# Two transformer layers on one core: whole-array jobs ahead of the values in TensorE's step

## What is computed

```python
xn = _layernorm(x)
x = x + _L0_attn_ref(xn, ...) + _L0_ffn_ref(xn, ...)
xn = _layernorm(x)
x = x + _L1_attn_ref(xn, ...) + _L1_ffn_ref(xn, ...)
```

## Time and profile before

| | |
|---|---|
| median of 3 runs | 901.5 us (899.99 to 901.91) |
| the profiled execution | 900.29 us, of which the profile's span is 897.3 us |
| TensorE, matmuls | 822.3 us busy, 92% of the span |
| TensorE, weight loads (beside matmuls) | 297.3 us, 33% |
| ScalarE | 762.6 us, 85% |
| VectorE | 540.9 us, 60% |
| GpSimd | 25.0 us, 3% |
| DMA | 76.07 MB, 85 GB/s on average |
| granted TensorE clock, mean | 0.966 |

### The profile page before, as it was taken

How to read it: one execution, slowest core, us unless ns; L and a number is a source line. 1 busy time by engine, 2 the same in 40 slices (tenths; PEclk the granted TensorE clock), 3 DMA queues, 4 the chain that set the end, 5 groups by cost and what they waited for, 6 DMA issues and landing times. The chain is left out here.

```text
span 897.3 us, 17912 instructions
## 1 busy us (share of the span) xinstructions
PE 822.3 (92%) x6815; PEld 297.3 (33%) x6815; DVE 540.9 (60%) x1193; ACT 762.6 (85%) x850; POOL 25.0 (3%) x39
## 2 busy tenths in 40 slices
PE   9568888899899999999899999999999789999996
PEld 7212222243233323333233323333233322333332
DVE  7165468675865567755866467846767167277321
ACT  1458998788989998899989998899988599899985
POOL 1000000000000000000000000000000000000000
PEclk9669998999999999999999999999999699999999
DMA  3663515533437307280246407280154604105100
GB/s 87 142 145 90 85 22 158 128 49 54 129 75 143 52 2 203 57 137 4 103 101 136 59 1 202 49 139 10 72 133 111 84 1 143 35 18 166 39 12 12
DMA packets 43889, 76.07 MB, mean 85 GB/s; under 512 B 6496, under 2 KB 8416, under 8 KB 43792
## 3 DMA queue, kind: packets, MB, share of 16 engines
q1 hardware_dynamic: 42492, 71.53, 36.1%
q10 hardware_dynamic: 668, 1.25, 0.8%
q0 software_dynamic: 640, 2.10, 0.7%
HBM read 37.37 MB, written 35.65 MB: 81 GB/s over the span
## 5 line engine op out<-in xcount | busy, mean ns | idle before, releaser
L664 ACT ACTIVATE probs<-ps_s 128x1024 f32<-128x1024 f32 x768 | 725.6, 1047 | 87.4 <-PE ps_s L810 87.0
L829 PE MATMUL ps_pv<-probs,v_aug 128*32 128x512 f32 x3072 | 419.4, 619 | 9.9 <-ACT probs L664 5.3
L810 PE MATMUL ps_s<-q_ab,k_ab 18*128 18x512 f32 (+1 forms) x1088 | 145.4, 507 | 35.3 <-ACT probs L664 23.1
L810 PEld LDWEIGHTS ps_s<-q_ab,k_ab 18*128 18x128 f32 (+1 forms) x1088 | 55.4, 186 | 207.7 <-ACT probs L664 165.8
L829 PEld LDWEIGHTS ps_pv<-probs,v_aug 128*32 128x32 f32 x3072 | 62.0, 109 | 119.0 <-issue 85.2
L689 PE MATMUL ps_misc<-h_hi,k_w 128*128 128x512 f32 x192 | 86.4, 450 | 2.6 <-DVE norm_max L1119 0.8
L810 PE MATMUL ps_s<-q_c,k_c 34*128 34x512 f32 x448 | 84.9, 453 | 0.0
L1217 DVE STREAM_TRANSPOSE pv_sb<-ps_pv 128x512 f32<-128x512 f32 x48 | 34.4, 716 | 71.6 <-PE ps_pv L829 68.5
L690 PE MATMUL ps_misc<-h_lo,k_w 128*128 128x512 f32 x192 | 76.6, 399 | 0.0
L1050 DVE CAST h_hi<-ff_out 128x512 fp32r<-128x512 f32 x64 | 27.3, 427 | 78.4 <-ACT ff_out L629 76.5
L689 PEld LDWEIGHTS ps_misc<-h_hi,k_w 128*128 128x128 f32 x192 | 36.3, 189 | 88.8 <-issue 45.2
(11 more groups left out here) (139 smaller groups left out, 555.0 us busy)
## 6 DMA issues: line engine op xcount, KB each, us to landing
parts_dram<-qk_parts SPq DMA_DIRECT2D x32, 512.0 KB, 3.4
parts_dram<-qk_parts SPq DMA_DIRECT2D x62, 256.0 KB, 4.0
q_ab<-parts_dram SPq DMA_DIRECT2D x64, 128.0 KB, 4.5
k_ab<-parts_dram SPq DMA_DIRECT2D x60, 128.0 KB, 5.9
q_c<-parts_dram SPq DMA_DIRECT2D x14, 512.0 KB, 7.6
k_c<-parts_dram SPq DMA_DIRECT2D x14, 512.0 KB, 9.0
x_all<-in_L_attn_x_dram SPq DMA_DIRECT2D x8, 256.0 KB, 6.5
out_dram<-x_all POOLq DMA_DIRECT2D x8, 256.0 KB, 6.7
```

The source lines that it names most:

```text
L664: nc.scalar.activation(probs[:, U.slot(s), 2 * half:2 * half + 2], ps_s[:, 2 * pair:2 * pair + 2], ACT.Exp, scale=SCALE[U.layer]).then_inc ...
L810: ins = nc.tensor.matmul(ps_s[:, bank, :], k[row:row + n, slot, c * P:(c + 1) * P], q[row:row + n, slot, :], start=True, stop=True)
L829: ins = nc.tensor.matmul(ps_pv[32 * j:32 * j + 32, :], v_aug[:, U.v, c, a:a + 32], probs[:, U.slot(s), j, :], start=c == 0 and not odd, st ...
```

## The change

In TensorE's program the jobs of a step are looked at before its values. In every unit but the first, the leading jobs that stand in the new list `WHOLE` are run between the scores and the values of the step; from the first job on that does not stand there, all stay behind the values. No table and no other engine's program is changed.

```diff
+WHOLE = ("x_t0", "x_t1", "quant_t", "ff_t", "w_t", "ff0", "ff1", "ff1_b", "ff2", "ff2_b")
...
                     items = TABLE[u].get(s, [])
                     exact = items and items[0][0] in ("exact0", "exact1")
                     holds = heads_within(int(items[0][0][-1]), items[0][1]) if exact else None
+                    jobs = [item for item in items if item[0] in TAKER or item[0] in ("exact0", "exact1")]
+                    n = 0
+                    while u > 0 and n < len(jobs) and jobs[n][0] in WHOLE:
+                        n += 1
+                    run(jobs[:n])
                     if s >= 2:
                         pv(U, s - 2)
                     elif u > 0:
                         pv(Unit(u - 1), STEPS - 2 + s)
-                    run(items, holds)
+                    run(jobs[n:], holds)
```

## The result

The changed kernel takes 919.99 us (median of 6 runs, 919.19 to 924.9) where the kernel before takes 901.14 (6 runs beside it, 899.99 to 902.23): ratio 1.022, 95% interval 1.0198 to 1.0242, slower. The forecast was 916.9, its likeliest case 911 to 922. The profiled execution took 924.9 us, of which the span is 922.2.

What follows compares the result with a forecast made beforehand. TensorE (92% busy) and ScalarE's exponentials take turns as the bound. Terms 2.0 + 1.3 + 4.5 + 0.9 + 7.8 - 1.1 = +15.4 us on the profiled 900.3 give 915.7; from the median 901.5, 916.9, range 905 to 926.

Steps and rivals of the forecast that it cites:

- the body of 103.9 to 104.1 us: Sign that the forecast is right: one loop body takes 103.9 to 104.1 us for 102.1.
- ff0 2, +0.9 five times: Loop body, step 4: its bank holds q1 until VectorE's shuffle ends, so job and values start late; 4.5 us in all.
- x_t1, +0.5 four times: Step 14 of C: the job waits for the normalised input and step 15's exponential has no reserve; 2.0 us in all.
- ff0 1, +0.25: Loop body, step 1: 0.6 idle until an activation empties its bank; +0.25 (0.15 to 0.4), five times, 1.3 us.
- ff1 1 and ff1 2, 0.2: Steps 14 and 0: the activation freeing the bank ends about 0.1 late; 2 x 0.1, five times, 0.9 to 1.0 us.
- The places that lose all of the cover: Outside the body, five jobs (three ff0, an x_t1, ff0 3) lose the whole cover of 1.0 us each.
- The seven shorter ones: Seven shorter losses outside the loop body, 0.1 to 0.8 us each, 2.8 together.
- Evictions on ScalarE, 0: The activations' 20.9 us wait for their jobs goes, but TensorE sets the exponential behind them, so nothing is gained.
- The rival that priced it as a gain, 896.0: ScalarE is what counts: the 20.9 us before the activations are on the path and come back, 896.0 us; chance 0.06.
- Tiling, 0 with ends of 16.7: Moved steps keep three changes of tiling, so 0; ends 111 x 0.15 = 16.7 us either way.
- ff1_b and ff_t in steps 1: They delay VectorE's take by 1.1 and 0.6, hidden by reserves; if those go, each costs up to 0.2 us.
- The case of the falling clock, 0.12: Rival: new idle time brings stretches at half clock, 1 to 3 us each; five to ten give 925 to 935; chance 0.12.

Runs made afterwards that it cites:

- the ready jobs alone: Kernel before, with only the 31 leading whole-array jobs whose bank and operands are ready in time moved (26 steps, units 5 to 17): 901.26 us, ratio 1.0008.
- ff1_b 2 alone: Kernel before, with only ff1_b 2 in step 1 of B moved ahead of the values (five times): 901.17 us for 899.92, ratio 1.0018.
- the copy first: Changed kernel, with VectorE's copy of x_t0 put ahead of the first part of the quantisation in step 3 of B: 916.85 us, ratio 1.0178.
- the steps 1 left as before: Changed kernel, but no job moved ahead of the values in any step 1 (15 steps): 911.85 us, ratio 1.0134.
- unit 1: Kernel before, with only x_t0 of unit 1, step 0 moved ahead of the values: 900.33 us, ratio 0.999.
- a close relative: Changed kernel, but ff0 2 of step 4 in five A units stays behind the values; run twice: 913.35 and 914.26 us, ratios 1.0146 and 1.0136.

## Why the prediction was right, and where not

The total was right (919.99 for 916.9, range 905 to 926), and so was the mechanism, time lost where a moved job waits with no values beneath it. Not all the terms were, and that the total came so close is in part luck: a missed term of 4.4 stands against terms that were 2.5 too dear. Of the signs named beforehand one failed, the body of 103.9 to 104.1 us (104.8); the others came.

- **ff0 2, +0.9 five times:** right, 0.89 each, the job at the end of the shuffle.
- **x_t1, +0.5 four times:** right, 0.57. **ff0 1, +0.25:** 0.36, inside its bounds. **ff1 1 and ff1 2, 0.2:** 0.17.
- **The places that lose all of the cover:** +0.89 in step 15 of units 2 and 19, +1.00 in unit 22, 0.84 in unit 4, 0.9 for ff0 3 in unit 17. Right. **The seven shorter ones**, 2.8 together, were too dear: the traces show some 1.6 at full clock, in units 4, 18, 20 and 21. One more, in step 9 of unit 20, shows as 0.69 in four kernels with a part undone, and not in either profile of the changed kernel, which has a fall of the clock 7 us before it.
- **Evictions on ScalarE, 0:** right. 15.2 of the 20.9 us went from ahead of the activations, and the exponentials' idle grew by 40.3. The rival that priced it as a gain, 896.0, is out.
- **Tiling, 0 with ends of 16.7:** right, by the ready jobs alone.
- **The term that failed: "ff1_b and ff_t in steps 1 delay VectorE's take behind them ... what hides that is a reserve".** I followed the take to the layer norm, found 0.7 of slack before x_t0 needs it, and stopped. The queue behind the take goes on: split, reciprocal, quantisation, then the copy out of x_t0's bank, on which q0 waits. That reserve was nothing. 0.88 for 0, at most 0.2, in five units: 4.4 us, shown by ff1_b 2 alone and by the copy first. ff_t's take cost 0.13 (C, step 3), within the bound. Unit 4 has a late take of its own, 0.34 by the steps 1 left as before.
- **A gain that I didn't see:** step 10 of A, -0.27 four times. The copy of v1's bank stands behind VectorE's split of ff0 3, and starts 1.40 after v1 before (444.47 to 445.87) and 1.13 after it in the changed kernel (457.56 to 458.69). That isn't the move of ff0 3. In the kernel with only ff0 2 behind the values again, ff0 3 is still moved, and the copy is as late as before, 1.40 after v1 (449.75), and the norm waits 1.09:

```profile
449.91 0.43 DVE L1057 CAST h_hi<-ff_out 128x512 fp32r<-128x512 f32 x1
...
451.15 0.69 DVE L1123 COPY v_aug<-ps_misc 128x512 f32<-128x512 f32 x1
...
451.90 0.39 PE L733 MATMUL ps_misc<-qk_sq,head_sel 128*32 128x512 bf16 x2 [1.09 <-DVE v_aug L1123]
```

It belongs to ff0 2: its 0.89 delays TensorE and the exponentials, but VectorE's rotation of q1 and k1 less, so that VectorE comes to the split of ff0 3 earlier against them (0.19 ahead of v1's start, 457.37, for 0.16 behind it). So ff0 2 cost 0.89 less 0.27 in four bodies.

Added up at full clock, with the loop's terms times their places: 2.3 (x_t1) + 1.8 (ff0 1) + 3.4 (ff0 2 less step 10) + 0.9 (ff1) + 0.4 (C) + 4.4 (B) + 6.4 (outside, for 7.8: 4.5 in the five places, 1.6 in the shorter ones, 0.3 behind unit 4's take) - 1.1 = 18.5, against 18.85 between the medians. So the forecast was 3.1 short: one missed chain of 4.4, for the greater part made up by the gain in step 10 (1.1) and by places outside the body that were too dear (1.4). The case of the falling clock, 0.12, came true in part: more falls, but outside the body. The six runs were at half clock for 66 us at the median, by span and granted clock, the two profiles for 76 and 62, and that of before for 61. Inside the body the clock stayed whole in both profiles of the changed kernel, in spite of waits of 1.03 in step 4 and 0.81 before the norm.

## What to carry to other kernels

In the program of an engine that works in order, as TensorE's does here, filler work (the values) belongs beneath a wait: between a job and the one that needs it, or ahead of a job whose bank or input comes late. Which tile shape stood first was no criterion here. Before a job is moved ahead of filler, compare the time at which its bank and its input are ready with the filler's start; only if both are there is the move free, and it gains only if something waits for its result. And when a move delays one instruction on another engine (a take), follow that engine's queue to the first result that someone waits for, not only the result that the instruction itself makes: here 0.87 of the 1.00 reached the exponential. Compare such kernels step by step in their traces where the clock is whole: here that tells 0.06 us, and the runs tell 2 to 3.

## What the runs showed of the hardware

In two profiles of the changed kernel, 4.9 us apart, the steps' exponentials add the same within 0.06 us from unit 4 to 16, where the granted clock is 1.00; the difference arises in the first 170 us, where the stretches at 0.50 lie differently (129.9 and 160.6 in the one, one of 17.1 us from 149.0 in the other). In the profile before, stretches at 0.50 sum to 61 us of 897. Three of the other kernels (the ready jobs, unit 1, ff1_b 2) have a short stretch at 0.50 in unit 5, steps 11 and 12, which costs each 1.6 us and which the changed kernel doesn't have. And falls late in the program seem not to be chance alone: at 751 us they came in both profiles of one kernel and in none of a close relative, behind waits of the same 1.19 us; of all fourteen profiles ten fall at that wait and four don't. So some 2.5 to 3.4 us between these two kernels' medians, found twice, are not in any step at full clock, and go with the time at half clock.
